# Layer 1's attention product by 64x64 quadrants in plain fp32, in a four-layer graph network on one NeuronCore

## The reference, cut to what matters

```
h = max(layernorm(x), 0)
query, keyt, value = h @ Wq.T + bq,  h @ Wk.T + bk,  h @ Wv.T + bv
weight = adj * exp(query @ keyt.T)                    # per graph, 64 x 64
weight = weight / sum(weight, axis=2)
x = x + weight @ value                                # per graph, 64 x 512
```

## Time and profile before

| | |
|---|---|
| time, median of 3 runs | 2355.19 us |
| the profiled execution: its time | 2355.34 us |
| its span | 2353.5 us |
| granted TensorE clock, mean | 0.997 |
| TensorE busy | 2319.0 us, 99% of the span |
| VectorE, ScalarE, GpSimd busy | 58%, 34%, 34% |
| layers 0 and 1, rounds 2 to 15 | about 132 to 857 us |
| layer 2 from | 891 us |

### The profile page before, as it was taken

The page is one execution under the profiler, slowest core; times in us unless marked ns, Lnnn a source line. Parts: engine busy times, 40 slices in busy tenths (PEclk is TensorE's granted clock), DMA queues, the critical chain, the costliest instruction groups (busy, mean ns, idle before and its releaser), DMA issues. The chain is left out here.

```text
span 2353.5 us, 39283 instructions
## 1 busy us (share of the span) xinstructions
PE 2319.0 (99%) x15823; PEld 1896.0 (81%) x15823; DVE 1355.4 (58%) x2602; ACT 797.0 (34%) x1429; POOL 807.1 (34%) x995
## 2 busy tenths in 40 slices
PE   8999999999999999999999999999989999999998
PEld 5788888888888887888888888888768888888887
DVE  3665656666556555444555444555677667676753
ACT  3433333343333433333333333333332222223221
POOL 2454444455445424223332222332442221212120
PEclk9999999999999999999999999999999999999999
DMA  6323333333333334222223222222434333334330
GB/s 195 79 72 93 106 99 88 93 81 82 90 93 111 101 117 114 59 59 59 65 80 91 59 60 59 65 77 89 130 97 111 84 105 86 103 86 107 83 89 36
DMA packets 173477, 208.97 MB, mean 89 GB/s; under 512 B 64800, under 2 KB 81264, under 8 KB 173296
## 3 DMA queue, kind: packets, MB, share of 16 engines
q1 hardware_dynamic: 173296, 206.48, 31.7%
HBM read 88.91 MB, written 50.37 MB: 59 GB/s over the span
## 5 line engine op out<-in xcount | busy, mean ns | idle before, releaser
L328 PE MATMUL bank<-w_hi,h3T_hi 128*128 128x512 f32 x768 | 302.8, 394 | 0.0
L328 PE MATMUL bank<-w_hi,h3T_lo 128*128 128x512 f32 x768 | 299.8, 390 | 0.0
L328 PE MATMUL bank<-w_lo,h3T_hi 128*128 128x512 f32 x768 | 299.8, 390 | 0.0
L613 DVE TENSOR_TENSOR Z_lo<-bank,Z_hi 128x512 fp32r<-128x512 f32 x128 | 87.1, 682 | 192.0 <-ACT Z_hi L956 191.9
L328 PEld LDWEIGHTS bank<-w_hi,h3T_hi 128*128 128x128 f32 x768 | 144.7, 188 | 30.2
L328 PEld LDWEIGHTS bank<-w_lo,h3T_hi 128*128 128x128 f32 x768 | 144.6, 188 | 30.2
L328 PEld LDWEIGHTS bank<-w_hi,h3T_lo 128*128 128x128 f32 x768 | 144.5, 188 | 30.1
L613 DVE TENSOR_TENSOR cT_lo<-bank,cT_hi 128x256 fp32r<-128x256 f32 x128 | 44.8, 410 | 203.7 <-ACT cT_hi L956 203.7
L956 ACT ACTIVATE Z_hi<-bank 128x512 fp32r<-128x512 f32 x128 | 76.0, 595 | 253.0 <-PE bank L328 163.3
L646 DVE STREAM_TRANSPOSE hs<-hn 128x512 f32<-128x512 f32 x192 | 123.4, 687 | 58.0 <-ACT hn L970 58.0
L1198 POOL TENSOR_SCALAR stA<-stA 128x4 f32<-128x4 f32 x48 | 11.9, 247 | 414.9 <-DVE stA L627 413.6
(11 more groups left out here) (231 smaller groups left out, 6050.0 us busy)
## 6 DMA issues: line engine op xcount, KB each, us to landing
hGA<-hs SPq DMA_DIRECT2D x768, 64.0 KB, 2.0
mid<-x SPq DMA_DIRECT2D x32, 1024.0 KB, 4.8
x<-mid SPq DMA_DIRECT2D x32, 1024.0 KB, 5.7
x<-in_x SPq DMA_DIRECT2D x16, 1024.0 KB, 5.9
hGB<-hs SPq DMA_DIRECT2D x256, 64.0 KB, 2.0
out<-x SPq DMA_DIRECT2D x16, 1024.0 KB, 5.5
blk<-in_adj SPq DMA_DIRECT2D x128, 64.0 KB, 3.1
adj<-in_adj SPq DMA_DIRECT2D x64, 64.0 KB, 3.8
```

Of the source, the lines that this page charges most:

```text
L328: ins = eng.matmul(b[:], h[l][:, k, ts], W[r][:, k, :], start=(k == 0 and i == 0), stop=(last and k == 3 and i == 2))
L613: return eng.tensor_tensor(lo, src, hi.bitcast(F), ALU.subtract)
```

## The change

The product of a tile is made in plain fp32 from `ext` and `vf` directly. The two graphs of a tile are on different partitions, and the 512 features are cut in two halves of 256, so there are four matmuls to a tile, each 64 rows by 64 columns of the array: graph 0 and 1 with the first half of the features, to the same half of the bank's partitions (line 378 after), and graph 0 and 1 with the second half of the features, each to the other half of the partitions (line 382 after). `vf` is now one tile [128, 4, 2, 264], whose column 256 of the first half is one, so that the first pair has 257 columns, and the last is the row sum. The first halves of a tile have a bank of their own (`pvx`); the second halves of two tiles share one (`pvy`). The splitting into `phi`, `plo`, `vv` hi and lo is gone from the ScalarE, the VectorE and the GpSimd, and so is `l01_sums`. On the VectorE one reciprocal and four updates of 128 x 512 become four reciprocals of one column, four updates of 128 x 256 and eight of 64 x 256.

```diff
-            def l01_sums(g):
-...
-                for t in range(4):
-                    for i, p in enumerate((phi, plo)):
-                        ins = eng.matmul(b[:, 2 * t:2 * t + 2], p[:, t, :], onesr[:], start=(i == 0), stop=(i == 1))
-...
-                    for i, (p, q) in enumerate(((phi, "hi"), (phi, "lo"), (plo, "hi"))):
-                        ins = eng.matmul(b[:], p[:, t, :], vv[q][:, t, :], start=(i == 0), stop=(i == 2))
-                    ins.then_inc(full, 1)
+                pe.wait_ge(p_ex, g + 1)
+                pe.wait_ge(v_vf, 4 * g + 4)
                 for t in range(4):
+                    bx, full_x, before = bank.take(("pvx", g, t), (v_x2, 12 * g + 6 * (t // 2) + t % 2 + 1))
...
+                    if t % 2 == 0:
+                        by, full_y, before = bank.take(("pvy", g, t // 2), (v_x2, 12 * g + 6 * (t // 2) + 6))
...
+                    for h in HALF:
+                        ins = eng.matmul(bx[h, 0:257], ex[h, t, :], vf[h, t, 0, 0:257], start=True, stop=True)
+                    ins.then_inc(full_x, 1)
+                    ys = slice(256 * (t % 2), 256 * (t % 2) + 256)
+                    for a, h in enumerate(HALF):
+                        ins = eng.matmul(by[HALF[1 - a], ys], ex[h, t, :], vf[h, t, 1, 0:256], start=True, stop=True)
+                    if t % 2:
+                        ins.then_inc(full_y, 1)
...
-                    eng.scalar_tensor_tensor(xt, bank.of(("pv", g, t))[:], rcol[:, t:t + 1], xt, ALU.mult, ALU.add).then_inc(v_x2, 1)
-...
-                eng.reciprocal(rcol, bank.of(("rs", g))[:, 0:8:2]).then_inc(v_rc, 1)
+                for u in range(2):
+                    for t in (2 * u, 2 * u + 1):
+                        dve.wait_ge(*bank.done(("pvx", g, t)))
+                        bx, x0 = bank.of(("pvx", g, t)), xg[:, t, 0:256]
+                        eng.reciprocal(rcol[:, t:t + 1], bx[:, 256:257]).then_inc(v_rc, 1)
+                        dve.wait_ge(v_rc, 4 * g + t + 1)
+                        eng.scalar_tensor_tensor(x0, bx[:, 0:256], rcol[:, t:t + 1], x0, ALU.mult, ALU.add).then_inc(v_x2, 1)
+                    dve.wait_ge(*bank.done(("pvy", g, u)))
+                    by = bank.of(("pvy", g, u))
+                    for t in (2 * u, 2 * u + 1):
+                        for a, h in enumerate(HALF):
+                            x1 = xg[h, t, 256:512]
+                            eng.scalar_tensor_tensor(x1, by[HALF[1 - a], 256 * (t % 2):256 * (t % 2) + 256], rcol[h, t:t + 1], x1,
+                                                     ALU.mult, ALU.add).then_inc(v_x2, 1)
```

More of the change, by code:

```diff
@@ L147, in build @@
         ident = alloc(root, "ident", [128, 128])
-        onesr = alloc(root, "onesr", [128, 2], R)
+        alloc(root, "pad0", [128, 2])
         small = alloc(root, "small", [128, 8])
@@ L193, in build @@
         gT.append(alloc(pa, "g1T", [128, 4, 512]))
-        phi, plo = alloc(pa, "phi", [128, 4, 128], R), alloc(pa, "plo", [128, 4, 128], R)
-        vv = pair(pa, "vv")
-        vf = [alloc(pa, f"vf{i}", [128, 512]) for i in range(2)]
+        unused1 = [alloc(pa, f"unused{i}", [128, 512]) for i in range(2)]
+        vf = alloc(pa, "vf", [128, 4, 2, 264])
         pa.close()
@@ L361, in l01_pt, with l01_pv @@
                 eng.transpose(b[:, 0:4], zrow[:], ident[0:4, 0:4]).then_inc(full, 1)
-            def l01_sums(g):
[L364 to L368, removed]
-                for t in range(4):
-                    for i, p in enumerate((phi, plo)):
-                        ins = eng.matmul(b[:, 2 * t:2 * t + 2], p[:, t, :], onesr[:], start=(i == 0), stop=(i == 1))
-                ins.then_inc(full, 1)
-            def l01_pv(g, ts):
-                for t in ts:
-                    b, full, before = bank.take(("pv", g, t), (v_x2, 4 * g + t + 1))
+            def l01_pv(g):
+                pe.wait_ge(p_one1, 1)
+                pe.wait_ge(p_ex, g + 1)
+                pe.wait_ge(v_vf, 4 * g + 4)
+                for t in range(4):
+                    bx, full_x, before = bank.take(("pvx", g, t), (v_x2, 12 * g + 6 * (t // 2) + t % 2 + 1))
                     if before:
                         pe.wait_ge(*before)
-                    pe.wait_ge(p_vlo, 4 * g + 4)
-                    pe.wait_ge(v_plo, 2 * g + 2)
-                    for i, (p, q) in enumerate(((phi, "hi"), (phi, "lo"), (plo, "hi"))):
-                        ins = eng.matmul(b[:], p[:, t, :], vv[q][:, t, :], start=(i == 0), stop=(i == 2))
-                    ins.then_inc(full, 1)
+                    if t % 2 == 0:
+                        by, full_y, before = bank.take(("pvy", g, t // 2), (v_x2, 12 * g + 6 * (t // 2) + 6))
+                        if before:
+                            pe.wait_ge(*before)
+                    for h in HALF:
[6 more added lines that the diff above has]
+                        ins.then_inc(full_y, 1)
             pe.wait_ge(c_pool, 1)
@@ L437, in pe_program @@
                 if on_pv:
-                    l01_sums(g - 2)
-                    l01_pv(g - 2, range(4))
+                    l01_pv(g - 2)
                 if on0:
@@ L545, in pe_program @@
                 else:
-                    l01_sums(NG - 1)
-                    l01_pv(NG - 1, range(4))
+                    l01_pv(NG - 1)
                 if on:
@@ L681, in l01_pt, with l01_x2 @@
                 eng.tensor_copy(pcol, bank.of(("pt", g))[:, 0:4]).then_inc(v_pcol, 1)
[L683 to L687, removed]
-                    eng.scalar_tensor_tensor(xt, bank.of(("pv", g, t))[:], rcol[:, t:t + 1], xt, ALU.mult, ALU.add).then_inc(v_x2, 1)
-            def l01_recip(g):
-                dve.wait_ge(*bank.done(("rs", g)))
-                eng.reciprocal(rcol, bank.of(("rs", g))[:, 0:8:2]).then_inc(v_rc, 1)
+            def l01_x2(g):
+                xg = xs[x_slot(kA(0, g))]
+                for u in range(2):
[12 more added lines that the diff above has]
+                                                     ALU.mult, ALU.add).then_inc(v_x2, 1)
             def l01_dots(g):
@@ L729, in dve_program @@
                 if on_pv:
-                    l01_recip(g - 2)
-                    l01_x2(g - 2, range(4))
+                    l01_x2(g - 2)
                 if g + 1 < NG:
@@ L771, in dve_program @@
                     for t in range(4):
[L772 to L775, removed]
                         dve.wait_ge(*bank.done(("v1", g - 1, t)))
                         dve.wait_ge(d_bv1, 16)
-                        dve.wait_ge(p_vlo, 4 * (g - 1) + t - 1)
-                        eng.tensor_tensor(vf[t % 2][:], bank.of(("v1", g - 1, t))[:], bv1[:], ALU.add).then_inc(v_vf, 1)
+                        if g >= 2:
+                            dve.wait_ge(*bank.done(("pvy", g - 2, 1)))
+                        b3, bias3 = (v[:].rearrange("p (c n) -> p c n", c=2) for v in (bank.of(("v1", g - 1, t)), bv1))
+                        eng.tensor_tensor(vf[:, t, :, 0:256], b3, bias3, ALU.add).then_inc(v_vf, 1)
                 else:
@@ L837, in dve_program @@
                 else:
-                    l01_recip(NG - 1)
-                    l01_x2(NG - 1, range(4))
+                    l01_x2(NG - 1)
                 stats_A(*(after2(g) if on else (3, 1)))
@@ L1061, in act_program @@
                         g1(g - 1)
-                    for t in range(4):
[L1063 to L1079, removed]
+                    act.wait_ge(*bank.done(("s1", g - 1)))
+                    act.wait_ge(v_ec, g)
+                    bv = bank.of(("s1", g - 1))
+                    for r in range(4):
+                        eng.activation(ex[:, r, :], bv[:, r * 64:(r + 1) * 64], ACT.Exp,
+                                       bias=ecol[(g - 1) % 2][:, 4 + r:5 + r]).then_inc(a_ex, 1)
             def l2_evict(n, g, dst, c0, done):
@@ L1244, in pool_program @@
                 if on1:
[L1245 to L1251, removed]
+                    pool.wait_ge(a_ex, 4 * g)
+                    pool.wait_ge(v_at, g)
+                    eng.tensor_tensor(ex[:], ex[:], atc[:], ALU.mult).then_inc(p_ex, 1)
                 else:
@@ L1256, in pool_program @@
                     pool.wait_ge(v_ucol, 1)
-                    for tl in (phi, plo):
-                        eng.memset(tl[:].bitcast(F), 0.0).then_inc(p_zero1, 1)
+                    eng.memset(vf[:, :, 0, 256:257], 1.0).then_inc(p_one1, 1)
             def s8(ap):
@@ L1512, in sp_program @@
                 if g == 0:
-                    sp.wait_ge(v_x2, 4 * NG)
+                    sp.wait_ge(v_x2, 12 * NG)
                     store_x(kA(0, NG - 1), mid[0][NG - 1])
```

14 lines of the change are left out of this document (6 added, 8 removed).

## The result

The changed kernel takes 2389.61 us (median of 4 runs) beside 2355.30 for the kernel before in the same session: ratio 1.0144, interval 1.0132 to 1.0157, 34 us slower. The profiled executions have spans of 2387.6 and 2353.5 us. The granted TensorE clock is 0.987 on average, where it was 0.997.

A forecast was written before the change was run, and what follows sets the result against it. TensorE, busy 99%, was taken as the bound, with the VectorE's chain to `wS` deciding each round after the change: 2355.34 + 1.4 (14 rounds) + 0 (group 14) - 1.5 (group 15) = 2355.2 us, range 2350 to 2366.

The forecast's parts named there:

- four quadrants at a time: TensorE's attention product: 32 records in 8 rounds of four, 2.16 us in place of 3.67, 1.5 us gained a group.
- the prediction's P: Start of the attention product's first matmul, from which the prediction counts a round's times; 445.21 us in round 8 before.
- the 10.08 us from the statistics to `wS`: Unheld chain in a round: statistics, GpSimd scales, ScalarE normalization, transpositions, lines 742 to 747; taken from round 3.
- rival (c): Attention product: quadrants run two at a time with 256 columns, product 3.9 us, only group 15 loses; 2357 us; chance 0.10.
- rival (a): At line 354 the TensorE doesn't wait, so its saving arrives: 2333 us, or 2345 for half; chance 0.10.
- the 0.44 us for the change of form: TensorE's way into and out of quadrant tiling, from layer 2's 1.30 us insertion with 0.86 for four at a time.
- Pitch 0.42 ... I take 0.42 for these too: VectorE's updates of `x`: 256-column updates start 0.42 us apart, those of 64 partitions too.
- 5.96 us: VectorE's reciprocals and updates from first reciprocal to statistics: 4 x (0.16 + 0.07 + 0.42) + 8 x 0.42.
- rival (b): Lines 688 to 696: first form, short updates don't overlap, pitch 0.48, +10 us, 2365; both forms together chance 0.20.
- The second form: Rival (b): half-partition updates slowed while GpSimd's `h1T_lo` runs beside them, 3 us a round, 2397 us.
- waits 1.6 us: TensorE at `l01_wt`, line 354, waits for the VectorE's chain once a round; round 0.1 us longer, +1.4 us over 14.
- the old wait for `h1T_lo`: Group 14, behind the transpositions of `q2w`: TensorE's existing 1.8 us wait for a GpSimd chain absorbs the 1.5 us saved.

The follow-up runs named there:

- e3: The changed kernel with `l01_wt` and `l01_pt` one tile of `l01_v0` later in the TensorE's order; 2329.99 us, 0.9880 to the kernel before.
- e2: The kernel before with only the VectorE's update of `x` cut as in the changed kernel, TensorE's product as before; 2372.56 us, 1.0063.
- e5: The changed kernel with a bank's four half-partition updates reordered, both of one half of `x` first, then both of the other; 2378.39 us, 1.0091.
- e1: The changed kernel with eight unused fp32r matmuls ahead of `l01_wt`'s wait for `wS` in rounds 2 to 15; 2369.91 us, 1.0047 to the kernel before.
- e7: The changed kernel with two unused matmuls ahead of `l01_wt`'s wait for `wS` in rounds 2 to 15; 2366.63 us, 1.0041.
- e8: The changed kernel with 512-column quadrant products, separate row-sum matmuls, and six wide updates in place of twelve; 2354.13 us, 0.9990 to the kernel before.
- e4: The changed kernel with a group's last four half-partition updates put behind the statistics on the VectorE; 2338.39 us, 0.9915 to the kernel before.

## Why the prediction was wrong

It put the change at 2355.2 us, with 2350 to 2366; 2389.6 was measured.

What held: the place of the new wait (`l01_wt` for line 749, 14 times); that the whole of the TensorE's saving would turn into it; four quadrants at a time (2.0 us for the product with its way in, where 2.16 had been counted; 1.6 us saved a group, shown by e3's round of 50.62 us, where 1.5 had been); the first reciprocal 0.79 behind the prediction's P (0.77 taken); the 10.08 us from the statistics to `wS`; rival (c) and rival (a) out. One figure beside the argument was misread: in layer 2, 3.4 us one at a time over 1.30 measured is 2.6 times the speed, not 3.2; and the 0.44 us for the change of form was a remainder, where here the whole product leaves 0.26 over 8 x 0.215. With what the Trainium skill says in "TensorEngine Tiling (Array Packing)", PSUM Bottleneck, named in the prediction, the trace agrees in so far as the VectorE's chain from the first reciprocal to the statistics went from 3.55 us to 6.75 and became what sets the round. But it grew because it was cut up, and in e3 the same chain holds nothing up.

The step that failed first is the pitch of the updates, "Pitch 0.42 ... I take 0.42 for these too". Those of 128 partitions have no follower of their own kind here, and those of 64 start 0.515 apart: 5.96 us was 6.75. The chain made a round 0.99 longer, not 0.1. This was rival (b) in its first form, which I had priced at +10 us, and both forms together had a chance of 0.20. The second form, a slowdown beside the GpSimd, is out: all 128 half-partition updates last 479 to 488 ns, though `h1T_lo` runs beside them (from 461.48 to 466.52 in round 8). e2 shows the cost of the cut without any change in the TensorE's program: 14 to 17 us. e5 shows that a part of it, 0.47 us a round, hangs on the order of the halves.

The step that failed by most was missing from the sum: "waits 1.6 us" was priced at its length. The wait was 2.4 us, and behind it the granted clock fell to its lower level, which took another 1.42 us a round, 20 us. e1 and e7 show it: with the same chain and the idle stretch cut to 0.5 or to 1.9 us, the clock stays at 1.00 and 20 to 23 us come back. The two errors are coupled: the 1.6 us of wait that I forecast are less than e7's 1.85, which cost only their length, so without the first error the second would probably not have shown; no run has 1.6 us in the rounds. So the bound of (b), "a tenth of a microsecond in this chain is 1.4 us of time", holds only while the clock does.

On clocks the Trainium skill, "TensorE: Matmul & The Clock Gate", Part 1, has a rule that speaks to this, that the full clock is held by activity and given up after idleness; I had looked only at the waits and not asked what a new one does to the clock. The trace agrees with its two levels: matmuls 0.43 us apart at the one and 0.23 at the other. It agrees in part with the loss after idleness: the clock fell behind every wait of the changed kernel's rounds, but e5 has the same wait with and without a fall.

A small step that failed: in group 14 I counted on the old wait for `h1T_lo` to take the saving. In its place there came a wait for a bank, which is freed by the sixth update of `x`. The TensorE of the changed kernel:

```profile
895.85 1.76 PE L294 MATMUL bank<-ident,k2w_raw 128*128 128x128 f32 x12
899.61 0.66 PE L294 MATMUL bank<-ident,k2w_raw 128*128 128x128 f32 x4 [2.00 <-DVE x L696]
900.18 0.50 PE L317 MATMUL bank<-h1T_hi,a_hi 128*128 128x512 f32 x1
```

The first matmul of `h1T` starts at P + 6.5, a microsecond sooner than before (P + 7.6), so some of the saving was there. But here too the clock fell: the matmuls that follow are 0.43 us apart for some 3 us from 901 on, and the stretch from 900.18 to group 15's product took 1.6 us more than before. I had weighed neither the later bank nor the clock for this place. The stretch of 2.00 us is the same in e1 and e7, and there the clock did not fall.

## What to carry to other kernels

When one engine is made faster, look for the instruction at which it next meets a result of another, and measure how long before that the result is ready; here it was 1.7 us, and a product 1.6 us shorter with a chain of updates 3.2 us longer overran it. Moving the reader one tile later (e3) turned a loss of 34 us into a gain of 25. An idle stretch on the TensorE is to be priced with what the clock may do after it (here 1.4 us on top of 2.4), and an update cut over the partitions can cost more than its columns say (here 0.52 us a step in place of 0.40).

## What the runs showed of the hardware that was not expected

A VectorE update of 256 columns from PSUM starts 0.40 us after the one before when both begin at the same partition, and 0.48 to 0.52 us, with no overlap, when the first partition changes (e2, and the changed kernel); grouping the halves gave back 0.47 us of 6.75 (e5). A change on one side is enough. In the changed kernel the step from 461.68 to 462.19 changes only the first partition of the bank that is read (0 to 64) and the bank, and costs 0.51; another bank alone costs nothing, since the updates before, each from a bank of its own, start 0.69 apart and last 0.75. In e5 the reciprocal at 462.47 reads from partition 0, as the update before it did, and only what is written moves from 64 back to 0; it starts 0.03 us after that update's end, where the reciprocal at 461.49 starts 0.07 before the end of the update ahead of it.

The granted clock fell behind every one of 14 idle stretches of 2.4 us in the changed kernel's rounds, behind none of 14 of 1.85 us in e7, and behind 12 of 14 of 1.92 to 1.93 us in e5. No length seen in this range decides by itself. In the kernel before, an idle stretch of 2.49 us that ends at 99.58 us has no fall behind it; stretches of 2.49 us at the same place in e1 and e8 have one. The 2.00 us behind group 14 brought a fall in the changed kernel, e3 and e4, and none in e1 and e7. In e2 the clock fell once, at 1695.4 us, with no idle stretch over 0.82 us in the 3 us before it, behind quadrant products of 64 columns.
